# Layer 1 of a two-layer kernel: how far routing runs ahead of attention, the pitch of the expert batches and the place of the final reads

## The reference

```python
xn = _layernorm(x)
x = x + _L1_attn_ref(xn, ...) + _L1_ffn_ref(xn, wg, we)

# _L1_attn_ref: 16 heads of 8 features, keys and queries through a latent
# projection, half of each head rotated (rope), causal softmax, then @ Wc
# _L1_ffn_ref: 128 experts, 32 slots each, over all 8192 tokens in order
logits = xt @ wg;  e1, e2 = best and second best expert of each token
loc1 = place of the token in the queue of e1
loc2 = its place in the queue of e2, behind ALL first choices of e2
buf[idx1] += xt * (loc1 < 32);  buf[idx2] += xt * (loc2 < 32)
yb = buf.reshape(128, 32, 128) @ we          # per expert
y = g1 * (loc1 < 32) * yb[idx1] + g2 * (loc2 < 32) * yb[idx2]
```

## Time and profile before

| | |
|---|---|
| median of 3 runs | 2108.28 us (2106.7 to 2112.17) |
| the profiled execution | 2114.91 us, span of its instructions 2113.1 us |
| granted TensorE clock, mean | 0.948 of full speed |
| PE busy | 1901.7 us (90%) |
| DVE busy | 1681.5 us (80%) |
| ACT busy | 1342.4 us (64%) |
| POOL busy | 1309.4 us (62%) |

### The profile page before, as it was taken

How to read it: one execution, slowest core, us unless ns; L and a number is a source line. 1 busy time by engine, 2 the same in 40 slices (tenths; PEclk the granted TensorE clock), 3 DMA queues, 4 the chain that set the end, 5 groups by cost and what they waited for, 6 DMA issues and landing times. The chain is left out here.

```text
span 2113.1 us, 41768 instructions
## 1 busy us (share of the span) xinstructions
PE 1901.7 (90%) x14386; PEld 1137.6 (54%) x14386; DVE 1681.5 (80%) x2731; ACT 1342.4 (64%) x2423; POOL 1309.4 (62%) x1008
## 2 busy tenths in 40 slices
PE   5789999999999999999999999994899999998985
PEld 3446555555565555555555555552455555555542
DVE  5588888798898987988989889774888888776655
ACT  3577776776767767777677677651355555554653
POOL 2477877877878778688787787753333333333650
PEclk8899999999999999999999999995899999998996
DMA  8733615426336064262461642606344444445558
GB/s 194 160 84 72 140 51 114 106 49 138 80 83 141 25 138 95 58 140 74 91 134 33 135 98 49 145 1 176 110 116 116 117 116 117 121 135 140 171 144 244
DMA packets 212029, 235.27 MB, mean 111 GB/s; under 512 B 31590, under 2 KB 150414, under 8 KB 207694
## 3 DMA queue, kind: packets, MB, share of 16 engines
q1 hardware_dynamic: 207116, 227.98, 44.3%
q0 software_dynamic: 2048, 4.18, 0.7%
q10 hardware_dynamic: 2640, 0.24, 0.1%
HBM read 165.51 MB, written 66.85 MB: 110 GB/s over the span
## 5 line engine op out<-in xcount | busy, mean ns | idle before, releaser
L738 POOL TENSOR_TENSOR dBx<-REP,BC 128x1024 f32<-128x1024 f32 x256 | 604.1, 2362 | 249.6 <-DVE dA L911 213.9
L911 DVE TENSOR_TENSOR_SCAN dA<-dA,dBx 128x512 f32<-128x512 f32 x512 | 626.5, 1224 | 143.1 <-POOL dBx L738 110.1
L406 PE MATMUL UP<-xnT,W 128*128 128x512 f32 x1024 | 520.8, 627 | 66.5 <-ACT hT L609 52.0
L415 PEld LDWEIGHTS DN<-W,hT 128*128 128x128 f32 x4096 | 471.4, 192 | 92.7 <-issue 83.4
L415 PE MATMUL DN<-W,hT 128*128 128x128 f32 x4096 | 494.1, 278 | 0.3 <-ACT GD L616 0.3
L600 ACT ACTIVATE dA<-REP,A 128x512 f32<-128x512 f32 x512 | 354.6, 696 | 81.3 <-DVE PR L920 74.0
L609 ACT ACTIVATE hT<-UP,b 128x512 f32<-128x512 f32 x512 | 356.3, 696 | 73.5 <-PE UP L406 61.4
L920 DVE TENSOR_TENSOR PR<-dA,BC 128x512 f32<-128x512 f32 x512 | 353.6, 691 | 33.6 <-DVE dA L911 20.9
L406 PEld LDWEIGHTS UP<-xnT,W 128*128 128x128 f32 x1024 | 182.9, 196 | 300.3 <-ACT hT L609 167.8
L1815 DVE TENSOR_REDUCE NM<-S 128x4 f32<-128x1024 f32 (+1 forms) x192 | 234.0, 1219 | 79.1 <-PE S L1360 78.9
L1574 ACT ACTIVATE PT<-S 128x1024 f32<-128x1024 f32 x192 | 197.1, 1027 | 95.3 <-PE S L1360 94.5
(11 more groups left out here) (254 smaller groups left out, 2669.1 us busy)
## 6 DMA issues: line engine op xcount, KB each, us to landing
BC<-s_b SPq DMA_DIRECT2D x128, 256.0 KB, 6.3
REP<-s_dx SPq DMA_DIRECT2D x124, 256.0 KB, 7.9
REP<-s_delta SPq DMA_DIRECT2D x124, 256.0 KB, 8.7
s_parts<-SPL SPq DMA_DIRECT2D x64, 192.0 KB
KS<-s_parts SPq DMA_DIRECT2D x64, 192.0 KB
QS<-s_parts SPq DMA_DIRECT2D x64, 192.0 KB
s_dx<-tz SPq DMA_DIRECT2D x16, 512.0 KB, 3.0
s_y<-zeros SPq DMA_DIRECT2D x32, 256.0 KB, 2.7
```

The lines of the kernel that those rows point to most:

```text
L406: nc.tensor.matmul(UP[k % 2][:], W1[:, e % E0, f * P:(f + 1) * P], xnT[:, q, :], start=True, stop=True).then_inc(upf.sem, 1)
L415: last = nc.tensor.matmul(DN[:, j * P:(j + 1) * P], hT[:, e % 2, f, j * P:(j + 1) * P], W2[:, e, f, :], start=(f == 0), stop=(f == FB - 1))
L738: nc.gpsimd.tensor_tensor(dBx[:, s % 2], DX[:, h, j:j + 2, :], BC[:, q // 2, q % 2, :].unsqueeze(1).to_broadcast([P, 2, T0]), ALU.mult).th ...
L911: nc.vector.tensor_tensor_scan(h, h, dBx[:, k // 2 % 2, k % 2, :], 0.0, ALU.mult, ALU.add).then_inc(scan_done.sem, 1)
```

## The change

It sets three constants. Routing runs up to eleven sequences ahead instead of seven, so `MAPPED` falls from slot 288 to 240, `GATHER` from 296 to 248, and the ring of `xnT` grows from 12 to 16 buffers. A batch starts every 12 slots (one per attention sequence) instead of every 10: the first gather stands at slot 248 and the last scatter at 343, where they stood at 296 and 377. The final reads start at slot 346 instead of 376; six of them and five additions stand before slot 392, beside the last sequences.

```diff
-AHEAD = 7
+AHEAD = 11
 RING = AHEAD + BUF + 1
...
     MAPPED = HS1 * (NSEQ - 1 - AHEAD)
     GATHER = MAPPED + 8
-    EVERY = 10
-    FINAL = (376, 378, 381, 384, 389, 392, 395, 398)
+    EVERY = HS1
+    FINAL = (346, 354, 362, 370, 378, 386, 391, 396)
```

## The result

The changed kernel takes 2152.96 us (median of 4 runs, 2146.88 to 2154.04) against 2110.23 us before (4 runs): ratio 1.0192, 95% interval 1.0172 to 1.0213. It is 43 us slower; forecast were 2159 us and a range of 2130 to 2178.

What follows compares the result with a forecast made beforehand. It took PE as full in quiet stretches, waiting on POOL then ACT in dear ones. Terms -195.4 + 26.4 + 177.1 + 51.9 + 0.6 + 4 - 13.5 = +51 us against 2108.3 gave 2159 us, range 2130 to 2178.

Steps and rivals of the forecast that it cites:

- Step 1: Attention stretches: four more at double-rate routing, eight fewer at single, seven old batch stretches gone; -195.4 us.
- Step 2: First gather and index lists, ahead of the batches: they move as they are, 26.4 us.
- Step 3: Seven scatter-and-gather stretches: closed loop through POOL, ACT and PE, 25.3 us each, 177.1 us in all.
- the bound of 23.3: Lower bound in us for each scatter-and-gather stretch, 17.3 plus a 6.0 us PE gap, if the clock stays up.
- Rival D: Scatter-and-gather stretches: the clock's full penalty makes each 27.5 us, +15 us, 2174 us in all; chance 0.05.
- Step 4: Three stretches with final reads instead of batches: 51.9 us, last scatter 0.6, delay of the maxima through HBM 4.
- Rival C: Last sequences: final reads stand ahead of the maxima's store, +13 to +21 us, 2172 to 2180 us; chance 0.12.
- Step 5: After the last sequence's first tile: PE gaps close as final reads move earlier; -13.5 us, ends -17 and -5.
- the bound of 17: Kernel's end: the most, in us, that closing its PE gaps could save.
- The sign of 43 to 48 us: Expected time from the last first tile to the end in the changed profile, instead of 59.5 us.
- Rival A: Scatter-and-gather stretches: the pair hides, 17.3 to 17.9 us each, some 2100 us in all; chance 0.08.
- Rival B: Scatter-and-gather stretches: partly hidden as ACT and PE catch up, 20 to 22 us each, about 2128 us; chance 0.1.

Runs made afterwards that it cites:

- e3: Changed kernel with the gather two slots earlier, ahead of the scatter of the batch before: 2098.7 us, ratio 0.9935 to the kernel before.
- e4: Changed kernel with the final reads at their old slots (376 to 398): 2157.2 us, ratio 1.0222 to the kernel before.
- e2: Changed kernel with POOL's scatter four slots later, behind the sum, pitch 12 kept: 2106.0 us, ratio 0.9978 to the kernel before.
- e1: Changed kernel with a batch every 10 slots again, all else kept: 2104.6 us, ratio 0.9973 to the kernel before.
- e10: Changed kernel with routing nine ahead, pitch 12, gather ahead of scatter, final reads from slot 368 on: 2101.2 us, ratio 0.9950.
- e3b: Repeat of e3, the same edit to the changed kernel, on the chip of the next two runs: 2099.8 us, ratio 0.9954.
- e6: Changed kernel with routing nine ahead, a batch every 10 slots, scatter four slots later, final reads from slot 362 on: 2102.9 us, ratio 0.9959.
- e7: Changed kernel with two of the four indirect DMAs of each gather left out: 2131.2 us, ratio 1.0089 to the kernel before.
- e5: Changed kernel with the edit of e3, final reads at slots 350 to 396 and stores 12 slots behind: 2105.7 us, ratio 0.9973.
- e8: Changed kernel with the edit of e2, final reads at slots 350 to 396 and stores 12 slots behind: 2107.6 us, ratio 0.9970.

## Why the prediction was right

**Step 1, the double rate**: four more stretches cost 83.2 us (83.5 forecast), eight fewer at the single rate 140.1 (140.1). That routing beside attention is nearly free at the single rate and not at the double one was the reading that made a gain unlikely: moving routing forward pays 3.5 us a sequence and gets 0.2 back.

**Step 2, the first gather**: 25.4 us for 26.4, within what this stretch varies by.

**Step 3, the loop**: 12.3 us from `YB` to `SPL` as forecast, a gap of 5.95 for 6.0. The stretch averages 24.6 for 25.3, within 23.3 to 26.1 but for one of 26.6. In six of the seven loops the clock was low for 6.8 us, which begin inside the gap; one such stretch of the clock:

```profile
1944.70:1951.50 6.80, 4.17 (x42) 2.31 (x46) 1.82 (x4) 3.70 (x6) 3.31 (x3) 0.50 0.24 68
```

What this costs is read against e3, which does the same work in these stretches with the clock up: there PE is busy for 16.22 us of 17.10 and idle for 0.88. In a stretch of 24.00 us PE is busy for 17.86 and idle for 6.14. The idle time grew by 5.26 us, which is the gap of 5.95 in place of 0.70, and the busy time by 1.6 us, which is the clock. The stretch of 26.60 us has PE busy for 20.56, so there the clock cost 4.3; a low stretch of 13.7 us had begun in the gap before it. Over the seven stretches 37 us are longer waiting and some 15 are the low clock behind it. So the forecast had the clock's share about right (2.0 us a stretch put in, 2.2 measured on average), and its overestimate of 0.7 us is in the other term: 17.3 + 6.0 counts the small wait twice that a quiet stretch has already. It is 17.1 + 5.3 = 22.4 us without any loss by the clock, below the bound of 23.3 that the forecast drew. Round the loop the same shows: from `SPL` to the end of the next `YB` 11.9 us passed, against 12.1 to 13.8 in its rows and 10.1 in e3.

By the rule of the Trainium skill ("TensorE: Matmul & The Clock Gate", Terms), half of the throttled time, 6.8 us would cost an estimated 3.4; the trace shows about half of that, 1.6. PE was waiting for 2.6 of the 6.8 us (until 1947.33) and busy for 4.17. Rival D falls with this.

**Step 4, the final reads**: 56.5 us for three stretches, measured 52.1. Two errors met here. The base of 17.3 a stretch was too high: e4 shows 48.5 without reads. And the reads cost 3.6 us, close to the 4 forecast, but not by way of the maxima: the wait is for the last parts. Rival C, at 13 to 21 us, did not come: no wait of line 1394 for `QS<-s_nm` of over 1.5 us is left.

The 8.28 us from which C was read were mostly not a transfer behind other transfers. SP's list in the kernel before:

```profile
2065.16 8.90 SPq L1312 DMA_DIRECT2D YC<-s_y  x6
2074.11 1.20 SPq L1296 DMA_DIRECT2D s_nm<-NMT  x1
```

ACT had the maxima ready at 2067.81. SP had waited for the last scatter until 2065.1, then issued six reads, the last two only when the first addition had given a buffer back, and issued the store 6.3 us late. Reads in flight make the store itself slower, but by less: in the changed kernel it lands in 1.4 us where no read stands ahead of it, and in 2.3 to 3.8 us behind reads and a store of tokens. So the order of transfers in one queue, on which C leaned, can be behind only this smaller part; the larger is SP standing in its own list, as in e2.

**Step 5, the end**: 10.3 us shorter for 13.5. e1, with the same reads, has an end of 42.7 us, 16.8 shorter than before and near the bound of 17. What the changed kernel lacks to that is 6.5 us. It had the clock low for 30.7 us of its end in one piece, e1 for 3.4 us at this place; that piece in the changed kernel, and the whole end of e1:

```profile
2101.70:2132.40 30.70, 28.68 (x273) 12.92 (x266) 16.46 (x22) 13.08 (x18) 0.00 (x0) 0.50 0.55 161
```

```profile
2058.50:2101.20 42.70, 28.97 (x400) 15.27 (x398) 24.55 (x36) 19.52 (x26) 0.00 (x0) 0.94 0.63 186
```

For the same 400 matmuls PE is busy for 39.5 us in the changed kernel's end and for 29.0 in e1's: 10.5 us more, of which 4 come out of its waits. Ten profiled executions with early reads (all but the kernel before, e4 and e10) go the same way: from 42.7 us with 5.2 us of low clock in the end (e1, e2) over 43.9 with 15.5 (e3b) to 49.2 with 35.2 (the changed kernel) and 50.4 with 36.8 (e6), 0.23 us for each us of low clock. That is a relation, from one profile each; what makes the clock stay low in some ends and not in others is not settled, nor that it is the change. Nor is all of the 10.3 us the work of the reads: e4, with the reads at their old slots, already has an end 4.5 us shorter than the kernel before, with 19.3 us of low clock in it against 33.4. The sign of 43 to 48 us that the forecast gave for the end was missed by 1.2 us. Of the eight pieces seven, not six, stand before slot 392; the one at 391 was counted rightly here, among the two behind the last second pass.

Sum: +54.0 in the stretches for +64.6 (steps 1 to 4), -10.3 for -13.5, which is 43.7 for 51. The medians moved by 42.7. Steps 2 to 4 were too dear by 10 us, and step 5, too hopeful, made up for 3 of them; that is luck. The sum was put on a median of 2108.3 us, which stands at 2110.2 with the fourth run; that brought the total 2 us nearer, luck again. The span of 2138 to 2168 is not what the ends of steps 3 to 5 give when all are taken together: the low ones give 2138, the high ones 2186.

Rival A was wrong by the point that it named: the pair hides when `SPL` comes 7 us behind `YB`, which e3 brought about. Rival B: PE's idle time grew by the whole of the longer gap, so no wait was made up.

## What to carry to other kernels

An engine that is 60% busy can set the pace if a wait and its long work stand in its queue ahead of a short step that others need: read where in its order the work stands, not how busy it is. Work that waits for nothing belongs ahead of work that waits, since it fills the wait; here two slots on one engine were worth 54 us. And locking two cycles to the same pitch makes their worst meeting permanent if the phase is wrong, and frees all of them if it is right; choose the phase first.

## What the runs showed that was not expected

- The gap of PE repeats to 0.04 us over seven loops and over kernels (5.94 to 5.98 us in the changed kernel, 5.95 to 5.96 in e4, 3.34 in four of the seven loops of e7): a loop of this kind can be forecast by addition.
- A low stretch of the clock of 6.8 us behind a PE gap of 6 us costs 1.6 us, since part of it falls on the gap. The low clock is also part of the scatter between executions of one kernel: of the 26 of the kernel before that were timed beside e5 to e8, the eight with a mean clock of 0.949 or less have a median of 2114.4 us, the ten with 0.953 or more one of 2108.6.
- The start of layer 1 wanders by 7 us between executions of programs that share layer 0. It is as large as the differences between the better kernels here, and only repeated runs tell those apart.
